# One core, a Mamba block, an attention and a mixture of experts: u reaches the scan by transfers, its product with B is made on GpSimd, the decay stays in PSUM

## The reference, cut to what matters

```
xh, z = split(x @ W_in);  xc = silu(causal_conv_2(xh))            # 128 inner channels
dt = softplus(xc @ W_x[:, :4] @ W_dt + b_dt);  Bm, Cm = xc @ W_x[:, 4:20], xc @ W_x[:, 20:]
h[t] = exp(dt[t] * A) * h[t-1] + dt[t] * Bm[t] * xc[t]            # 128 channels x 16 states, 1024 steps
y = sum over states of h[t] * Cm[t] + xc * D;  x = silu(group_norm((y * silu(z)) @ W_out)) + x
t = t + attention(layer_norm(t))                                  # 8 heads of 8, causal, 1024 tokens
t = t + top_2_of_8_experts(layer_norm(t))                         # router softmax, 8 linear experts
```

## Time and profile before

| | |
|---|---|
| median of 3 runs (lowest to highest) | 1472.35 us (1471.16 to 1510.57) |
| profiled execution: time, span, mean granted clock of TensorE | 1472.47 us, 1470.7 us, 0.844 of full speed |
| busy in the span | PE 76%, DVE 78%, ACT 48%, POOL 33% |
| a turn with everything in it | 160.4 us (from 556.78 to 717.21, POOL line 648) |

### The profile page before, as it was taken

One profiled execution on the slowest core, in us unless ns is written; L12 is line 12 of the kernel. 1 busy time (PEld: TensorE's weight loads), 2 busy tenths in 40 slices (PEclk: granted clock), 3 DMA queues, 4 the chain that ended last, 5 costly groups with the idle time before them and its releaser, 6 DMA issues.

```text
span 1470.7 us, 17619 instructions
## 1 busy us (share of the span) xinstructions
PE 1120.9 (76%) x6288; PEld 461.6 (31%) x6388; DVE 1154.0 (78%) x1427; ACT 703.6 (48%) x1298; POOL 485.9 (33%) x260
## 2 busy tenths in 40 slices
PE   4266367769886898789877988689878877886994
PEld 1011102323342333333333334233333333432442
DVE  5594597897699888898898979988889889259235
ACT  2334332458444764276436654477437621660660
POOL 2162353534353333343254335243335321000000
PEclk9557557889987999799978998799979997899796
DMA  1200330211311112201330121101220121030000
GB/s 43 50 1 14 95 57 15 54 29 34 62 47 35 29 32 59 66 1 34 70 79 3 34 62 44 46 14 34 50 73 2 34 55 37 4 74 7 4 15 8
DMA packets 25966, 55.29 MB, mean 38 GB/s; under 512 B 8582, under 2 KB 8970, under 8 KB 23499
## 3 DMA queue, kind: packets, MB, share of 16 engines
q1 hardware_dynamic: 25878, 54.15, 16.2%
HBM read 28.54 MB, written 13.00 MB: 28 GB/s over the span
## 4 chain that ended last, share of the span: by engine, by line
PE 31%; DVE 25%; issue 15%; POOL 6%; ACT 6%; another core or an unknown queue 1%; DVEq 0%; POOLq 0%; ACTq 0%
DVE row_max L955 11%; POOL read L687 6%; DVE state L1029 5%; PE ps L1424 5%; PE ps L1291 5%; PE ps L1409 4%; PE ps L1183 4%; PE ps L1194 3%; PE ps L1340 3%; PE ps L1203 2%; ACT probs L830 2%; PE ps L1188 2%; DVE drive L1038 2%; PE ps L1393 1%; PE ps L1295 1%
## 5 line engine op out<-in xcount | busy, mean ns | idle before, releaser
L687 POOL TENSOR_TENSOR read<-state,c_rep 128x1024 f32<-128x1024 f32 x128 | 303.6, 2372 | 438.7 <-DVE state L1029 344.9
L830 ACT ACTIVATE probs<-ps 128x512 f32<-128x512 f32 (+3 forms) x768 | 326.9, 498 | 108.4 <-PE ps L1412 76.5
L955 DVE TENSOR_REDUCE row_max<-ps 128x1 f32<-128x640 f32 (+7 forms) x352 | 334.4, 988 | 54.9 <-PE ps L1295 52.4
L1291 PE MATMUL ps<-k_stack,q_stack 128*128 128x512 bf16 (+3 forms) x672 | 209.7, 391 | 77.2 <-DVE row_max L955 73.2
L791 ACT ACTIVATE decay<-ps,a_scale 128x512 f32<-128x512 f32 x256 | 177.4, 697 | 151.4 <-PE ps L1340 127.9
L1029 DVE TENSOR_TENSOR_SCAN state<-decay,drive 128x1024 f32<-128x1024 f32 x96 | 245.3, 2556 | 1.2 <-POOL read L687 1.0
L1409 PE MATMUL ps<-q_stack,k_stack 128*128 128x512 bf16 (+3 forms) x727 | 202.4, 345 | 25.6 <-DMA q_stack<-max_parts_dram 12.5
L1340 PE MATMUL ps<-dt_rows,pick 128*128 128x512 bf16 x229 | 106.5, 465 | 88.3 <-DVE state L1014 40.4
L1424 PE MATMUL ps<-probs,v_aug 128*32 128x512 f32 (+3 forms) x1536 | 167.8, 509 | 4.4 <-ACT acc_sb L819 1.7
L1038 DVE TENSOR_TENSOR drive<-ps,b_rep 128x512 f32<-128x512 f32 x192 | 130.0, 680 | 51.9 <-PE ps L1340 51.8
L1409 PEld LDWEIGHTS ps<-q_stack,k_stack 128*128 128x128 bf16 x768 | 76.3, 102 | 220.5 <-ACT probs L830 95.4
(11 more groups left out here) (185 smaller groups left out, 1370.4 us busy)
## 6 DMA issues: line engine op xcount, KB each, us to landing
q_stack<-q_parts_dram SPq DMA_DIRECT2D x48, 192.0 KB
k_stack<-k_parts_dram SPq DMA_DIRECT2D x48, 192.0 KB
dt_rows<-read SPq DMA_DIRECT2D x96, 64.0 KB, 2.0
u_rows<-read SPq DMA_DIRECT2D x96, 64.0 KB, 2.0
k_parts_dram<-read SPq DMA_DIRECT2D x40, 128.0 KB, 2.4
q_parts_dram<-read SPq DMA_DIRECT2D x24, 128.0 KB, 2.2
xs<-in_x SPq DMA_DIRECT2D x8, 256.0 KB, 3.6
residual<-in_x SPq DMA_DIRECT2D x8, 256.0 KB, 9.6
```

Source lines behind the costliest of these rows:

```text
L687: pool.tensor_tensor(read[:, k % (2 * NG), :], state[:, k % 2, :], c_rep[:, :], ALU.mult)\
L830: act.activation(probs[:, e % (2 * QUAD), 0:w], bank_of(("scores", e))[:, 0:w], ACT.Exp, scale=SCALE).then_inc(exped.sem, 1)
L955: dve.tensor_reduce(row_max[:, i, h0:h0 + nh], scores[:, :, 0:P * (i + 1)], AX.X, ALU.max, negate=True).then_inc(row_maxed.sem, 1)
L1291: last = pe.matmul(ps[:, bank, 0:w], q_stack[:, h0 + hh, tokens(i)], k_stack[:, h0 + hh, h * BANK:h * BANK + w], start=True, stop=not diag ...
```

## The change

u is no longer split into parts and spread by PE. SP stores it to DRAM (`u_dram`), and one transfer of 512 KB for each chunk reads 8 rows of it sixteen times into one of seven `drive` buffers (`spread_u`); SP issues the first three behind dt's parts, four more behind q's and k's, ACT the other nine. The product with B is made in place over a whole chunk (`make_drive`): by POOL, two chunks ahead of its read, except that in the full turns DVE makes chunk 7 and in turns 1 and 2 the odd ones. The exponential is written back to dt's PSUM bank, which is free only when the half scan that reads it is done; all scans are halves, with the decay from PSUM and the drive from SBUF. Experts' weights are turned once at the start so that the sum over experts reads neighbours. `decay` and `u_rows` go, the three tables move a few entries (one unit from round 9 to 6, some experts later), xc's step moves from 9 to 7 and the group scale's from 17 to 15.

```diff
-decay = sb("decay", [P, 2, T])
-drive = sb("drive", [P, 3, T])
+drive = sb("drive", [P, DRIVES, T])   # DRIVES = 7
...
-UNITS_IN = (4, 0, 2, 1, 1, 1, 2, 0, 2, 1, 2, 2, 0, 2, 1, 1, 0, 0, 1, 1, 2, 1, 2, 1, 0, 1, 0, 1)
+UNITS_IN = (4, 0, 2, 1, 1, 1, 3, 0, 2, 0, 2, 2, 0, 2, 1, 1, 0, 0, 1, 1, 2, 1, 2, 1, 0, 1, 0, 1)
+FOLDS = ((0, 0, 12), (0, 1, 7), (1, 0, 20), (1, 1, 18))
+POOL_DRIVES = (0, 1, 2, 3, 4, 5, 6, 8, 9, 10, 11, 12, 13, 14, 15)
+POOL_IN_FILL = (0, 2, 4, 6, 8, 10, 12, 14)
+DRIVE_AHEAD = 2
+SPREAD_LAG = 3
+FIRST_SPREADS = 3
...
-return {"early": (row_maxed, p), "dt": (decayed, c), "u": (driven, c) if b else (scanned, c), ...
+return {"early": (row_maxed, p), "dt": (scanned, c), ...
...
+def spread_u(engine, c, k):
+    rows = u_dram[c.number, CH * chunk(k)[2]:CH * (chunk(k)[2] + 1), :]
+    engine.dma_start(drive[:, k % DRIVES, :], rows.unsqueeze(0).to_broadcast([NS, CH, T]))\
+          .then_inc(u_in[k % DRIVES].sem, 16)
+def drivers(c, b):
+    if b:
+        return POOL_DRIVES, pool_drove, dve_drove
+    return POOL_IN_FILL, fill_pool_drove, fill_dve_drove
...
+def make_drive(engine, c, k, drove):
+    arrived = u_in[k % DRIVES]
+    engine.wait_ge(arrived.sem, arrived.at(c, 16 * (k // DRIVES + 1)))
+    engine.tensor_tensor(drive[:, k % DRIVES, :], drive[:, k % DRIVES, :], b_rep[:, :], ALU.mult)\
+        .then_inc(drove.sem, 1)
...
@@ SyncE @@
+for r, part_ready in enumerate((high_part, mid_part, low_part)):
+    sp.wait_ge(part_ready.sem, part_ready.at(c, 1))
+    hold(sp, "sp")
+    for g in range(NG):
+        sp.dma_start(dt_rows[32 * r:32 * (r + 1), g, :],
+                     part[r][GW * g:GW * (g + 1), :]).then_inc(dt_rows_in.sem, 16)
+    if r == 0:
+        sp.wait_ge(u_ready.sem, u_ready.at(c, 1))
         hold(sp, "sp")
-        for g in range(NG):
-            sp.dma_start(rows[32 * r:32 * (r + 1), g, :],
-                         part[3 * n + r][GW * g:GW * (g + 1), :]).then_inc(arrived.sem, 16)
+        sp.dma_start(u_dram[c.number, :, :], u).then_inc(u_stored.sem, 16)
+sp.wait_ge(u_stored.sem, u_stored.at(c, 16))
+hold(sp, "sp")
+for k in range(FIRST_SPREADS):
+    spread_u(sp, c, k)
...
@@ SyncE, behind the q and k parts' stores @@
+if c:
+    for k in range(FIRST_SPREADS, DRIVES):
+        spread_u(sp, c, k)
...
@@ GpSimd @@
+by_pool, drove, _ = drivers(c, b)
 if c:
+    pool.wait_ge(b_copied.sem, b_copied.at(c, 1))
+    for k in by_pool:
+        if k < DRIVE_AHEAD:
+            make_drive(pool, c, k, drove)
     pool.wait_ge(c_copied.sem, c_copied.at(c, 1))
-    if p:
-        pool.wait_ge(qk_parts_out.sem, qk_parts_out.at(p, 16 * 8))
+    pool.wait_ge(u_stored.sem, u_stored.at(c, 16))
 for k in range(NJ):
     if c:
+        if p and k == 2:
+            pool.wait_ge(qk_parts_out.sem, qk_parts_out.at(p, 16 * 8))
+        if k + DRIVE_AHEAD in by_pool:
+            make_drive(pool, c, k + DRIVE_AHEAD, drove)
...
@@ ScalarE @@
-if k >= 2:
-    act.wait_ge(scanned.sem, scanned.at(c, NH * (k - 1)))
 j = chunk(k)[2]
-act.activation(decay[:, k % 2, halves(h)], bank_of(("dt", k2)), ACT.Exp,
-               scale=a_scale[:, j:j + 1])\
-   .then_inc(decayed.sem, 1)
+act.activation(bank_of(("dt", k2)), bank_of(("dt", k2)), ACT.Exp,
+               scale=a_scale[:, j:j + 1]).then_inc(decayed.sem, 1)
+if h == 0 and k >= SPREAD_LAG and k - SPREAD_LAG + DRIVES < NJ:
+    act.wait_ge(scanned.sem, scanned.at(c, NH * (k - SPREAD_LAG + 1)))
+    spread_u(act, c, k - SPREAD_LAG + DRIVES)
...
@@ VectorE @@
 def scan_half(k2):
     k, h = k2 // 2, k2 % 2
     dve.wait_ge(decayed.sem, decayed.at(c, k2 + 1))
-    dve.wait_ge(driven.sem, driven.at(c, k2 + 1))
-    if h == 0 and k >= 2:
-        dve.wait_ge(read_out.sem, read_out.at(c, k - 1))
-    if h:
+    if h == 0:
+        wait_driven(dve, c, b, k)
+        if k >= 2:
+            dve.wait_ge(read_out.sem, read_out.at(c, k - 1))
+    else:
         dve.wait_ge(scanned.sem, scanned.at(c, k2))
-    dve.tensor_tensor_scan(state[:, k % 2, halves(h)], decay[:, k % 2, halves(h)],
-                           bank_of(("u", k2)), state[:, k % 2, BANK - 1:BANK] if h else 0.0,
+    dve.tensor_tensor_scan(state[:, k % 2, halves(h)], bank_of(("dt", k2)),
+                           drive[:, k % DRIVES, halves(h)],
+                           state[:, k % 2, BANK - 1:BANK] if h else 0.0,
                            ALU.mult, ALU.add).then_inc(scanned.sem, 1)
...
+def scan_unit(k2):
+    k, h = k2 // 2, k2 % 2
+    if h == 0 and k not in by_pool:
+        make_drive(dve, c, k, drove)
+    scan_half(k2)
...
-dve.tensor_reduce(moe_out[:, n, :], moe[:, n % 2, :, :].rearrange("p e c -> p c e"),
-                  AX.X, ALU.add).then_inc(combined.sem, 1)
+dve.tensor_reduce(moe_out[:, n, :], moe[:, n % 2, :, :], AX.X, ALU.add)\
+   .then_inc(combined.sem, 1)
```

159 lines of the change are left out of this document (67 added, 92 removed).

## The result

The changed kernel takes 1516.2 us (median of four runs) against 1472.3 before: ratio 1.0306, 95% interval 1.029 to 1.0323 (the ratio leaves out one slow run of the kernel before, 1510.6 us). That is slower by 44 us, outside the range given. The profiled execution's span is 1516.8 us against 1470.7. Nearly all of the extra 46 us lies in the full turns. The last product with values of turn 3 ends at 386.0 (383.1 before), the first full turn is 3.4 us longer, the other four 9.7 to 11.0 us each, and what follows them is 1.4 us shorter.

The account below looks back on a forecast made before the run. DVE was taken to bind the first half of the rounds, PE the second. Full turns +4, turn 3 -5, turns 1 and 2 +7, the end -3: +3 us on 1472.47, forecast 1475 us, range 1405 to 1508.

Parts of the forecast that it names:

- The exclusion: DVE operations with both inputs in SBUF and POOL's operations exclude each other; half scans from PSUM are not stretched.
- The start: Start of the rounds: last row maxima steps wait for POOL's third product, 2.9 us later, given back by the root.
- The spreads delay the maxima: Rival, chance 0.13: four spreads ahead of the maxima on SP's queue make scores 6 us late in six turns, 1511.
- Rounds 4 to 11: POOL's products and reads set the pace; scan 8 ends at 655.5; the first half gains a chunk and no time.
- The signs named for being wrong: Wrong if POOL idles in rounds 4 to 11, or if any half scan stretches beside POOL.
- The gates: Four POOL operations get between the gate operations, which take 12.3 us; round 14's product with values comes 5.8 us late.
- Rounds 14 to 27: Rounds behind the gates take 36.9 us, 5.1 saved; 1 or 2 us may go again after PE's stand.
- The score part: Loses two splits, two casts and twelve small transfers beside the row maxima that bind there: nothing gained.
- turn 3: Turn without gates: POOL's reads and products and PE's rounds end at about 377.5; 5 us saved.
- the fill: Turns 1 and 2: a pair of chunks takes 8.3 us against 7.74; together with changed starts +7 us.
- the end: Turn 11: eight sums over experts on the chain save 3 us, or nothing.
- The rival of no backlog: Chance 0.38: POOL has caught up at the gates, which take 3.4 us; five turns gain 44 us, 1431.

Follow-up runs that it names:

- the last run of the repairs with reads ahead: Changed kernel with products 0 to 2 before q and k's split, old xc and group-scale places, seven-bank ring, products three chunks ahead, reads before products: 1480.3 us, 1.006.
- the held run: Changed kernel with GpSimd waiting ahead of its read of chunk 8 until VectorE's gates are done: 1483.4 us, 1.0086.
- the other repairs: Changed kernel with products of chunks 0 to 2 before q and k's split, xc and group scale at old places, seven-bank ring: 1481.9 us, 1.0076 together.

## Why the prediction was wrong

**The exclusion was right.** Every two-SBUF operation of VectorE that began inside one of GpSimd's lasted until that ended; half scans from PSUM never did (all 256 lasted 1.20 to 1.28 us). Casts of the row maxima, which have one SBUF input, were held up too (1.00 us at 790.31, 0.20 before). The Trainium skill, "SBUF — State Buffer", section "Who interferes with whom", says that a VectorE instruction with two SBUF inputs contends with a GpSimd instruction that reads SBUF, over a port pair that is an exclusive lock; the gates' 2.46 and 2.20 us agree.

**The start** was right: the maxima 2.9 us late, given back up to the root (+2.9, -2.6). It was the cast and the first subtraction that waited (line 979's place, 2.30 us), not line 984's. **The spreads delay the maxima** did not happen: PE's first score comes 11.8 us after the last part of the maxima in the kernel before (623.3) and 11.5 after; the four spreads take 11.6 us, not the 8.5 or 6.8 worked out there, and land 1.5 us before the maxima leave. That the measured time lies near that rival's 1511 is chance.

**Rounds 4 to 11 is the step that failed.** I had GpSimd set the pace, with scan 8 done 25.0 us after the root; it is done 30.7 after. GpSimd's own part came as forecast: read 6, the last that scan 8 needs, ends 21.6 us after the root (22.5 forecast). But scan 8 starts 6.5 us later, when ACT's exponential is there, and scan 6 waits for its exponential too:

```profile
826.86 1.22 DVE L1064 TENSOR_TENSOR_SCAN state<-ps,drive 128x512 f32<-128x512 f32 x1 [3.86 <-ACT ps L840]
...
829.77 2.37 POOL L737 TENSOR_TENSOR read<-state,c_rep 128x1024 f32<-128x1024 f32 x1 [0.27 <-DVE state L1064]
...
838.63 1.22 DVE L1064 TENSOR_TENSOR_SCAN state<-ps,drive 128x512 f32<-128x512 f32 x1 [2.33 <-ACT ps L840]
```

So from scan 6 on the pace is not GpSimd's. The signs named for being wrong could not show it: GpSimd idled only 1.5 us from the root to the gates, and no half scan stretched.

What the step left out is that a scan needs an exponential, the exponential a spreading, and the spreading a bank that only an earlier half scan frees: DVE idles until ACT's exponential, PE until DVE's scan. GpSimd starts one round of it, since read 2 stands behind chunk 4's product. Then PE stands 4.17 us, and its granted clock is 0.72 from 816 to 822, behind it. PE's product for the router starts 22.2 us after the root in this turn, before the change 17.8. Reads ahead of products alone bring it to 20.8 to 21.1, two banks more alone to 22.1, both together (the last run of the repairs with reads ahead) to 18.6 in three of five turns, 19.6 and 20.0 in the others: both belong to the cause. Of the 6.4 us 3.8 are left in that run, and 2.2 of them lie in VectorE's list: the router's result is ready at 650.9 and taken up at 653.1, as VectorE's own product of chunk 7, stretched from 1.2 to 3.1 us beside GpSimd's read, and scan 7 stand ahead of it; before the change it was taken up at once. No run moved that product, so its price is not shown. The time kept little of this: 6 us in five turns with chunk 4's product on VectorE, nothing with the reads ahead.

**The gates** were mis-sized: two of GpSimd's operations got in, not four, 7.5 us instead of 12.3, because GpSimd had no backlog but waited 2.28 us for a fold just before. The two errors nearly cancel: the gates end 38.3 us after the root, forecast 37.3. Both come from the late scans; that they are of one size is chance. In the table's turn the forecast was off by 5.8 us up to the gates, -4.8 in them, 5.2 behind them and 2.5 in the score part, so the number itself was missed mostly by the next two terms.

**Rounds 14 to 27** were mis-sized by as much: forecast 36.9 us from the first product with values to the last, 5.1 less than before, measured 41.5. The 1 or 2 us allowed for the clock are there (1.4 by the held run). From the third product with values on, at full clock, the rounds take 36.0 us in the changed kernel and 36.2 in the held one; turn 9 of the changed kernel takes 29.1 for the same products, and ten spreadings and two folds (4.1) make 33.2. PE's waits for half scans, 0.2 to 0.8 us each, are 1.7 of the 2.8 left; they were put at nothing. What the rest is remains open.

**The score part** was put at nothing and costs 2.5 us in four turns: xc behind the gate, PE's stand, the clock (shown by the run with xc's old place).

**The small terms**: turn 3 gained 0.5 us, not 5; the fill lost 3.3, not 7, though a pair of chunks takes 8.5 us, forecast 8.3 (the start was 8 us earlier in turn 1); the end gained 1.4, not 3.

The range went wrong with the sign. Each case in it took the sum's other terms as they were, and none had a loss in the rounds that did not come from GpSimd. The rival of no backlog had its condition right, DVE held back and GpSimd caught up, but priced only the shorter gates and not their later start.

## What to carry to other kernels

A short chain of small operations on VectorE that others wait for must not lie beside GpSimd's long ones: find a place for GpSimd's work on both sides of it and hold GpSimd there, which here was worth 33 us alone and 31 us on top of the other repairs. When a PSUM bank is to be held longer, ask what else the ring serves: the wait goes to whoever takes the next bank, here PE, whose granted clock was 0.72 behind its stand of 4.17 us. A busy share that falls on the engines that were full while the time rises says that a chain through several of them binds; price its steps, not the engines.
